# Expert weights stored by expert and partition, and loaded in two transfers instead of three

## The reference

```python
fe = topk_idx.reshape(-1)                 # expert of each (token, choice), 65,536 in all
order = jnp.argsort(fe, stable=True)
tok = order // K
sorted_x = xf[tok]
g = jax.lax.ragged_dot(sorted_x, gate_w, group_sizes)      # gate_w (64, 512, 256)
u = jax.lax.ragged_dot(sorted_x, up_w, group_sizes)        # up_w   (64, 512, 256)
h = jax.nn.silu(g) * u
o = jax.lax.ragged_dot(h, down_w, group_sizes)             # down_w (64, 256, 512)
o = o * w.reshape(-1)[order][:, None]
routed = jnp.zeros_like(xf).at[tok].add(o)
```

## Time and profile before

| | |
|---|---|
| median of 3 runs | 5693.62 us (5679.9 to 5696.86) |
| profiled execution | 5680.15 us, of which the span of the instructions is 5678.4 us |
| TensorE busy | 5460.8 us, 96% of the span |
| mean granted TensorE clock | 0.986 |
| DMA, whole span | 836.06 MB, mean 147 GB/s |
| stage e | about 2690 to 5345 us of the span |

### The profile page before, as it was taken

One profiled execution on the slowest core, in us unless ns is written; L12 is line 12 of the kernel. 1 busy time (PEld: TensorE's weight loads), 2 busy tenths in 40 slices (PEclk: granted clock), 3 DMA queues, 4 the chain that ended last, 5 costly groups with the idle time before them and its releaser, 6 DMA issues. The chain is left out here.

```text
span 5678.4 us, 102617 instructions
## 1 busy us (share of the span) xinstructions
PE 5460.8 (96%) x33072; PEld 4563.9 (80%) x33072; DVE 3866.1 (68%) x7136; ACT 2592.0 (46%) x3737; POOL 3006.4 (53%) x2620
## 2 busy tenths in 40 slices
PE   8999979999999999998999999999999999999799
PEld 7888866666666666665899999999999999999686
DVE  5444437887778877776666666666666666666557
ACT  3222223333333333333666666666666666666310
POOL 2222212555555555411677777777777777777414
PEclk9999989999999999999999999999999999999899
DMA  6555454344444443432667677677787667676548
GB/s 223 181 180 177 170 151 128 110 121 122 115 136 125 114 129 112 127 114 92 146 112 155 133 140 160 134 154 162 177 210 169 133 138 151 133 156 112 135 169 284
DMA packets 478099, 836.06 MB, mean 147 GB/s; under 512 B 54273, under 2 KB 159490, under 8 KB 475251
## 3 DMA queue, kind: packets, MB, share of 16 engines
q1 hardware_dynamic: 337011, 541.90, 30.0%
q0 software_dynamic: 140928, 292.13, 28.6%
HBM read 501.55 MB, written 332.30 MB: 147 GB/s over the span
## 5 line engine op out<-in xcount | busy, mean ns | idle before, releaser
L1579 POOL DMA_INDIRECT mid_base<-e_rows,e_ox x556 | 1174.8, 2113 | 364.4 <-POOL e_ox L1574 254.4
L1687 DVE TENSOR_TENSOR e_wgu_lo<-e_wgu,e_wgu_hi 128x2048 fp32r<-128x2048 f32 x278 | 637.4, 2293 | 813.5 <-ACT e_wgu_hi L1611 730.5
L1567 POOL DMA_INDIRECT e_xg<-mid_xn,e_ix x556 | 624.4, 1123 | 338.6 <-POOL e_ix L1564 227.7
L1624 ACT CAST e_xT_hi<-e_ps_t 128x512 fp32r<-128x512 f32 x556 | 299.1, 590 | 917.2 <-PE e_ps_t L1752 911.9
L934 POOL DMA_INDIRECT mid_ids<-b_pairs,b_cell x512 | 616.5, 1204 | 148.8 <-issue 146.1
L1765 PE MATMUL e_ps_g<-e_xT_hi,e_wgu_hi 128*128 128x256 f32 x2224 | 653.5, 294 | 12.6 <-issue 12.5
L1765 PE MATMUL e_ps_g<-e_xT_lo,e_wgu_hi 128*128 128x256 f32 x2224 | 630.5, 283 | 0.0
L1765 PE MATMUL e_ps_g<-e_xT_hi,e_wgu_lo 128*128 128x256 f32 x2224 | 630.3, 283 | 0.0
L1765 PE MATMUL e_ps_u<-e_xT_hi,e_wgu_hi 128*128 128x256 f32 x2224 | 629.6, 283 | 0.0
L1765 PE MATMUL e_ps_u<-e_xT_lo,e_wgu_hi 128*128 128x256 f32 x2224 | 629.6, 283 | 0.0
L1765 PE MATMUL e_ps_u<-e_xT_hi,e_wgu_lo 128*128 128x256 f32 x2224 | 629.5, 283 | 0.0
(11 more groups left out here) (243 smaller groups left out, 13437.3 us busy)
## 6 DMA issues: line engine op xcount, KB each, us to landing
b_q<-mid_q_hi SPq DMA_DIRECT2D x128, 256.0 KB
b_xT_hi<-mid_xT_hi SPq DMA_DIRECT2D x32, 1024.0 KB
b_xT_lo<-mid_xT_lo SPq DMA_DIRECT2D x32, 1024.0 KB
mid_base<-b_x SPq DMA_DIRECT2D x32, 1024.0 KB, 6.5
c_cell<-mid_base SPq DMA_DIRECT2D x128, 256.0 KB, 5.2
e_wgu<-in_gate_w SPq DMA_DIRECT2D x62, 512.0 KB
e_wgu<-in_up_w SPq DMA_DIRECT2D x62, 512.0 KB
e_wd<-in_down_w SPq DMA_DIRECT2D x62, 512.0 KB
```

The source lines that it names most:

```text
L1567: pool.indirect_dma_start(xg[s][:, i, :], None, t["xn"], bass.IndirectOffsetOnAxis(ap=ix[s][:, i:i + 1], axis=0))\
L1579: pool.indirect_dma_start(t[f"base{i}"], bass.IndirectOffsetOnAxis(ap=ox[s][:, i:i + 1], axis=0), rows[s][:, i, :], None, compute_op=ALU.a ...
L1624: act.copy(xT_hi[s][:, i * DC // 2 * RB:(i + 1) * DC // 2 * RB], ps_t[i][:, :]).then_inc(xT_hi_ready, 1)
L1687: dve.tensor_tensor(wgu_lo[s][:, :], wgu[s][:, :], wgu_hi[s][:, :].bitcast(F32), ALU.subtract)\
```

## The change

The host arranges the expert weights so that for each expert and partition all bytes lie together: gate and up in one tensor `gu_w` of shape (64, 128, 2048), down as (64, 128, 1024). Gate and up are loaded by one transfer of 1 MB with 8 KB per partition, and down by one of 512 KB with 4 KB per partition. `gu_in` goes up by 16 for each block instead of 32. The arrangement on the host is not part of the time. The layout of the data in on-chip memory stays the same, and so does everything that reads it.

```diff
                 with sp.If(e != before):
                     load_gu(e, s)
                 with sp.Else():
-                    sp.sem_inc(gu_in[s], 32)
+                    sp.sem_inc(gu_in[s], 16)
...
             def load_gu(e, s):
-                for i, src in enumerate((t["gate_w"], t["up_w"])):
-                    sp.dma_start(wgu[s][:, i * DC * HID:(i + 1) * DC * HID].rearrange("p (k h) -> p k h", h=HID),
-                                 src[bass.ds(e, 1), :, :].rearrange("a (k p) h -> p (a k) h", p=P)).then_inc(gu_in[s], 16)
+                sp.dma_start(wgu[s][:, :], t["gu_w"][bass.ds(e, 1), :, :].rearrange("a p n -> (a p) n")).then_inc(gu_in[s], 16)
 
             def load_d(e, s):
-                sp.dma_start(wd[s][:, :].rearrange("p (k c) -> p k c", c=DIM),
-                             t["down_w"][bass.ds(e, 1), :, :].rearrange("a (k p) c -> p (a k) c", p=P)).then_inc(d_in[s], 16)
+                sp.dma_start(wd[s][:, :], t["down_w"][bass.ds(e, 1), :, :].rearrange("a p n -> (a p) n")).then_inc(d_in[s], 16)
...
             def split_gu(b, s, turn, first=False):
-                act.wait_ge(gu_in[s], turn * 32 + 32)
+                act.wait_ge(gu_in[s], turn * 16 + 16)
...
+    def expert_rows(w):
+        e, n, r, c = w.shape
+        return np.ascontiguousarray(w.reshape(e, n, r // P, P, c).transpose(0, 3, 1, 2, 4)).reshape(e, P, n * r // P * c)
...
-        gate_w=a(L0_ffn_gate_w), up_w=a(L0_ffn_up_w), down_w=a(L0_ffn_down_w),
+        gu_w=expert_rows(np.stack([a(L0_ffn_gate_w), a(L0_ffn_up_w)], 1)), down_w=expert_rows(a(L0_ffn_down_w)[:, None]),
```

## The result

The changed kernel takes 5723.91 us (median of 5 runs, 5713.58 to 5726.66), beside 5693.6 us for the kernel before (5 runs): a ratio of 1.0052, 95% interval 1.004 to 1.0064. It is slower by some 30 us. The forecast was 5690 us, and its range ended at 5722. The profiled execution of the kernel before (5680.15 us) was one of its quickest and that of the changed kernel stands at its median, so differences between these two profiles are rather too large than too small.

A forecast was written before the change was run, and what follows sets the result against it. TensorE in stage e was taken as the bound, touched by weights only through late gathers. -5.4 + 4.7 + 1.2 = +0.5 us on 5680.15 gave 5680.7; 10 added for run spread, forecast 5690 us, range 5672 to 5722.

The forecast's parts named there:

- What bounds the kernel: Stage e: TensorE sets the pace, busy 2385.65 of 2400 us; weights touch time only through 18 gather waits, 14.1 us.
- Issue, semaphores, splits at 0: Stage e loads: 62 fewer DMA instructions of 0.45 us covered by SP's waiting, same semaphore event, same split reads; 0.
- Speed of a load: Stage e loads: 0.65 us less engine time each; 0.3 us for each of 18 late gathers, -5.4 us.
- How the two queues share an engine: Stage e, weights beside gathers: split stays by bytes, 18 late gathers each wait 0.26 us longer for one larger piece, +4.7 us.
- the upper bound: Stage e: a pair of gathers behind all of gate and up ends 1.1 us later; up to +66 us less slack.
- the first rival: Stage e: gathers starve behind long pieces, 0.4 us per load, +24 plus 2.6 at the start, about 5717 us; chance 0.22.
- Start of stage e: First two gathers against the first two loads: 0 if split by bytes, 2.6 us later if weights go first; +1.2 taken.
- Starved gathers: Another name for the first rival: stage e gathers delayed behind long weight pieces, about 5717 us; chance 0.22.
- its own sign: Stage e profile after: TensorE's wait for gathered rows with over 40 entries and 30 us would show the first rival right.

The follow-up runs named there:

- no_reload: Changed kernel in which only the first two blocks load expert weights, leaving out 60 loads; ratio 0.9975 to the kernel before.
- the second pair: The kernel before and the changed kernel, both unedited, profiled once more; 16.0 and 33.3 us of waits for gathered rows, ratio 1.0043.
- halves_8k: Changed kernel with gate and up loaded as two transfers of 64 partitions each, still in 8 KB pieces; ratio 1.0134 to the kernel before.
- one_1k: Changed kernel with gate and up in one transfer cut into 1 KB pieces, and down in 2 KB pieces as before; ratio 1.0016 to the kernel before.
- the repeat: The changed kernel run once more, unedited; ratio 1.0043 to the kernel before.

## Why the prediction was wrong

*What bounds the kernel.* Right: only waits for gathered rows changed in stage e, and `no_reload` shows that loads cause them all. TensorE has no wait for weights in the changed kernel's loop.

*Issue, semaphores, splits at 0.* Nothing in the profile speaks against it. That a single transfer of 1 KB pieces costs 10 us was not in the prediction, though; joining two transfers was costed by its issue alone.

*Speed of a load.* The load became cheaper, 11.9% to 10.8% of the engines' time, where about 10% was forecast. Its worth of -5.4 us was not seen. `no_reload`, with no loads at all, is 13 us faster, so no relief could have brought more.

*How the two queues share an engine.* This is the step that failed: "I take +4.7, because both rows with the two queues in one stretch are nearest to a split by bytes." The rows compared 1 KB pieces with the gather's, and a split that is by bytes at that size need not stay so. Measured was +20.0 us of waits in the profile, and +20 to +26 us of the loop between the profiles. Two things were wrong in the term. First, it gave a gather beside a load 0.26 us more, one piece in service. The packets show 1.1 us more in the first pair of profiles (6.6 to 7.7) and 0.8 in the second (7.0 to 7.8), which is near the upper bound that the term had named (1.1) and then left. Second, it counted the 18 late gathers alone. Gathers that had been on time became late: 18 waits to 32, and 26 to 38 in the second pair. This is the part that I had left to the first rival.

How the engines came to serve the gathers later is less clear. Over all the microseconds of the loop in which a gather and gate and up each moved over 60 KB, the packets give some 0.7 bytes of gather for each byte of weights in the kernel before and 0.6 in the changed one. The value moves with the place where the microseconds are cut: 0.68 to 0.73 and 0.59 to 0.61 in the first pair of profiles, 0.74 to 0.80 and 0.58 to 0.74 in the second. It is thus much nearer to a split by bytes than to four pieces to one, which would give 0.12. In `halves_8k`, with the longest waits, it is 0.76 to 0.90. So the average split explains the loss at best in part. That the pairs end later is shown, and the turns within an engine are not.

The Trainium skill (DMA: Bandwidth & Descriptors, Queues, rings and completion order) has a queue keep its turn for a whole packet. By that rule the trace agrees in direction: the gathers ended later, and the first rival is what happened. No run here shows the turns themselves. The same page (SWDGE vs HWDGE vs iDMA) calls packets of at most 4096 B preferable, for the descriptors that GpSimd builds; here 4 KB pieces cost 0.24% and 8 KB pieces 0.43 to 0.52%, so the runs show a growing cost and no step at 4 KB that the intervals would prove. Its advice of at least 1 MiB per DMA for the most bandwidth (Rules for kernel authors) is not what made the load cheaper here: `one_1k`, with 1 MB in one transfer of 1 KB pieces, kept the weights at 11.7% of the engines' time, and the kernel lost 0.16%.

*Start of stage e.* +1.2 taken, +1.7 measured: the first wait is 26.9 us in both profiles of the kernel before and 28.6 in both of the changed one. Why it grew was not tried.

*The rivals.* Starved gathers had a chance of 0.22 and 5717 us. It named what happened, gathers that end later and use up the slack of those on time. Its price was near, +27 forecast and +30 measured (+24 in the repeat), but partly by luck. It took 0.4 us of TensorE's time for every load, while a gather beside a load came some 0.8 to 1.1 us later, and slack hid more than half of that. Of its own sign, over 40 waits and 30 us, only the second came true (32 waits, 34.1 us). What I held against it, that weights which finish sooner leave the engines to the gather, did not carry, and no row had shown it. With 18 of 60 gathers late already, on which any added delay counts in full, 0.22 was too little for it.

*Open.* Why one transfer of 1 KB pieces is slower than two is not settled, nor whether 2 KB pieces are better or worse than 1 KB: waits and ratios disagree there, and the late pairs (5 and 4, beside 2 and 6) show no difference. How an engine divides its turns was only seen in its results. Why 64 partitions take twice the time per piece was not tried by itself.

## What to carry to other kernels

Cheaper transfers are worth nothing where transfers aren't the bound, and longer pieces are not free to others: price them by what else waits on the same DMA engines, first of all by transfers that are late already. Look for the transfer with the least slack, count how often it is late, and take each added delay in full for those. Moving the lead of one such transfer may only hand the delay to the next one in its queue, so name that one before counting the gain. And count what follows a wait: TensorE's clock can fall after long ones, as in `halves_8k`.

## What the runs showed of the hardware

A transfer of 8 KB pieces into 64 partitions takes 600 ns per piece, one into 128 partitions 309. With 1, 2, 4 and 8 KB, the median piece of the weights takes 46, 84, 159 and 309 ns, that is 22, 24, 26 and 27 bytes per ns: each doubling wins less. After some of TensorE's waits of 2.1 to 3.1 us the granted clock stood at half (0.50): one stretch in the loop of the changed kernel, 48 us in all in `halves_8k`, none in the two profiles of the kernel before, whose longest wait was 2.3 us. The same program took 5661 us on three chips and 5685 on a fourth, and 5694 where the result was taken. Much of this arose before stage e, which began at 2678 to 2690 us on the three and at 2704 to 2722 on the others.
